# A ViT tower on one core: norms in two pieces, first tiles on the rounded input, and next query and key weights split at another place

## The reference, cut to what matters

```python
def t5_layer_norm(x, w):
    var = jnp.mean(x * x, axis=-1, keepdims=True)
    return w * x * jax.lax.rsqrt(var + EPS)
...
for i in range(L):
    nx = t5_layer_norm(h, ln1[i])
    q = (nx @ attn_q[i]).reshape(b, s, H, DK)
    k = (nx @ attn_k[i]).reshape(b, s, H, DK)
    v = (nx @ attn_v[i]).reshape(b, s, H, DK)
    scores = jnp.einsum('bqhd,bkhd->bhqk', q, k) + bias
    attn = jax.nn.softmax(scores, axis=-1)
    ctx = jnp.einsum('bhqk,bkhd->bqhd', attn, v).reshape(b, s, H * DK)
    h = h + ctx @ attn_o[i]
    nx = t5_layer_norm(h, ln2[i])
    y = jax.nn.relu(nx @ ffn_wi[i]) @ ffn_wo[i]
    if i in MOE_LAYERS:
        y = y + moe_ffn(nx.reshape(-1, d), gate_w[mi], moe_w1[mi], moe_w2[mi]).reshape(b, s, d)
        mi += 1
    h = h + y
return t5_layer_norm(h, ln_f)
```

## Time and profile before

| | |
|---|---|
| median of 3 runs | 741.36 us (739.84 to 741.7) |
| the profiled execution | 745.19 us, of which 743.4 us is the span from its first to its last instruction |
| PE busy | 678.4 us, 91% of the span, 6658 matmuls |
| DVE, ACT, POOL busy | 446.8, 405.0, 351.7 us |
| mean granted clock of PE | 0.963 |
| chain that ended last, by engine | PE 63%, DVE 11%, ACT 9%, POOL 8%, DMA 4%, issue 3% |

### The profile page before, as it was taken

The page is one execution under the profiler, slowest core; times in us unless marked ns, Lnnn a source line. Parts: engine busy times, 40 slices in busy tenths (PEclk is TensorE's granted clock), DMA queues, the critical chain, the costliest instruction groups (busy, mean ns, idle before and its releaser), DMA issues.

```text
span 743.4 us, 16264 instructions
## 1 busy us (share of the span) xinstructions
PE 678.4 (91%) x6658; PEld 609.8 (82%) x6658; DVE 446.8 (60%) x941; ACT 405.0 (54%) x914; POOL 351.7 (47%) x329
## 2 busy tenths in 40 slices
PE   6879979799889999999899989998899999999995
PEld 4757857588768888999899878787688898999994
DVE  0483567275475677565566655853856775666664
ACT  1486655534364374776675455444543647767642
POOL 2755275742573561547674424426734514553510
PEclk9998779988999999999999999989999999999998
DMA  9210100400221122434444110002211124333200
GB/s 256 75 48 7 40 1 2 118 2 1 77 74 44 33 72 64 134 109 128 134 118 122 42 45 2 2 1 75 76 44 33 61 75 134 90 104 107 75 1 23
DMA packets 36769, 49.20 MB, mean 66 GB/s; under 512 B 6315, under 2 KB 27735, under 8 KB 36183
## 3 DMA queue, kind: packets, MB, share of 16 engines
q1 hardware_dynamic: 33259, 43.49, 20.3%
q10 hardware_dynamic: 3436, 4.67, 2.1%
HBM read 47.70 MB, written 0.45 MB: 65 GB/s over the span
## 4 chain that ended last, share of the span: by engine, by line
PE 63%; DVE 11%; ACT 9%; POOL 8%; DMA 4%; issue 3%; ACTq 1%; SPq 0%; POOLq 0%; DVEq 0%
PE pd L716 31%; PE pa L716 21%; PE ps L716 7%; PE pa L747 4%; POOL prob L649 3%; POOL w L640 3%; ACT wide L1057 2%; DMA gate<-in_gate_w_dram 2%; DVE xn L1143 1%; DVE mx L1097 1%; ACT pa L1058 1%; DVE prob L1265 1%; POOL prob L655 1%; DVE xs L1109 1%; DVE xs L1107 1%
## 5 line engine op out<-in xcount | busy, mean ns | idle before, releaser
L640 POOL TENSOR_TENSOR w<-raw,w 128x384 fp32r<-128x384 f32 x140 | 141.7, 1014 | 126.3 <-ACT w L968 118.4
L716 PE MATMUL pd<-wide,w 128*128 128x264 f32 x1200 | 157.8, 288 | 0.1
L716 PEld LDWEIGHTS pd<-wide,w 128*128 128x128 f32 x1200 | 151.0, 190 | 1.0 <-DVE wide L1288 0.9
L716 PE MATMUL pa<-xs,w 128*128 128x264 f32 x810 | 121.2, 290 | 12.3 <-DVE wide L1288 8.1
L716 PEld LDWEIGHTS pa<-xs,w 128*128 128x128 f32 x810 | 107.7, 191 | 16.8 <-DVE wide L1288 10.2
L1288 DVE TENSOR_TENSOR wide<-pa,wide 128x264 fp32r<-128x264 f32 x144 | 62.0, 432 | 42.3 <-ACT pa L1058 40.2
L649 POOL TENSOR_TENSOR prob<-prob,mx 66x792 f32<-66x792 f32 x36 | 54.3, 1511 | 57.4 <-DVE mx L1097 57.1
L1057 ACT ACTIVATE wide<-pa 128x264 fp32r<-128x264 f32 x144 | 56.9, 395 | 38.1 <-PE pa L716 38.0
L655 POOL TENSOR_TENSOR prob<-prob,rc 66x792 f32<-66x792 f32 x36 | 54.3, 1511 | 45.1 <-DVE rc L1103 45.1
L716 PE MATMUL ps<-xs,w 128*128 128x264 f32 x480 | 74.2, 285 | 0.6 <-DVE prob L1265 0.6
L1179 DVE TENSOR_TENSOR pd<-pd,vtok 128x264 f32<-128x264 f32 x64 | 43.6, 681 | 41.5 <-PE pd L716 41.3
(11 more groups left out here) (139 smaller groups left out, 1101.0 us busy)
## 6 DMA issues: line engine op xcount, KB each, us to landing
raw<-in_moe_w_dram SPq DMA_DIRECT2D x16, 576.0 KB, 4.1
raw<-in_moe_w_dram SPq DMA_DIRECT2D x16, 384.0 KB, 3.5
raw<-in_moe_w_dram SPq DMA_DIRECT2D x32, 192.0 KB, 4.0
vtok<-cw_rows ACTq DMA_DIRECT2D x4, 1056.0 KB, 6.1
raw<-in_attn_o_dram SPq DMA_DIRECT2D x4, 576.0 KB, 4.0
raw<-in_ffn_wo_dram SPq DMA_DIRECT2D x4, 576.0 KB, 4.1
vtok<-in_patches_dram SPq DMA_DIRECT2D x2, 768.0 KB, 7.9
raw<-in_attn_q_dram SPq DMA_DIRECT2D x4, 384.0 KB, 3.8
```

Of the source, the lines that this page charges most:

```text
L640: ins = nc.gpsimd.tensor_tensor(low, whole, high.bitcast(F32), ALU.subtract)
L716: return nc.tensor.matmul(out_ap, lhsT, rhs, start=first, stop=last)
```

## The change

Three things are changed, and the number of matmuls on data stays the same.

1. A stage `tail_squares` stands ahead of `squares` in twelve norms: ACT squares the tail when its sum with the tail's part of the output is made, and the main part later; PE sums the tail's three pieces first and waits once more ahead of the main part's three.
2. `first_products` takes the place of the first three tiles of every `qk` for queries and of the first three of a layer's first hidden block: it claims three banks, runs the two matmuls of each tile that need only the rounded main input (a new semaphore `hi_ready`, signalled by the rounding), then waits for `x_ready` and runs the other three of each tile.
3. In layers 0 and 2 the rounding (`high`) of the next layer's query and key weights goes ahead of `scale` of the second norm, and their remainders (`low`) right behind it; the number of fillers changes from 1, 3, 6 to 2, 2, 3, 4 around it.

```diff
             yield ("o_main", 0, layer)
+            yield ("tail_squares", 0, "ln2")
             yield ("squares", 0, "ln2")
-            yield from warm(1)
+            yield from warm(2)
             yield ("pv", 1, layer, 1)
             yield ("tp", 1, layer, 2)
             yield ("norm", 0, "ln2", layer)
+            yield from warm(2)
             yield ("pv", 1, layer, 2)
             yield ("tp", 1, layer, 3)
+            yield ("high", None, "qkv", layer + 1, 0)
+            yield ("high", None, "qkv", layer + 1, 1)
             yield from warm(3)
             yield ("scale", 0, "ln2", layer)
+            yield ("low", None, "qkv", layer + 1, 0)
+            yield ("low", None, "qkv", layer + 1, 1)
             yield ("pv", 1, layer, 3)
-            yield from warm(6)
+            yield from warm(4)
             yield from hid(0, layer, 0)
-            yield ("split", None, "qkv", layer + 1, 0)
             yield from y(0, layer, 0)
...
             yield ("norm", 0, "ln1", layer + 1)
-            yield ("split", None, "qkv", layer + 1, 1)
             yield from warm(4)
...
+            def first_products(banks, w_hi, w_lo, hf, scale_stage, full):
+
+                n, x = x_ready_after(scale_stage), xs[hf]
+                tiles = [(bank, slice(m * 128, (m + 1) * 128)) for m, bank in enumerate(banks)]
+                pe.wait_ge(hi_ready, n)
+                for bank, cols in tiles:
+                    mm(bank, w_hi[:, 0, cols], x[:, 0], True, False)
+                    mm(bank, w_lo[:, 0, cols], x[:, 0], False, False)
+                pe.wait_ge(x_ready, n)
+                for bank, cols in tiles:
+                    mm(bank, w_hi[:, 0, cols], x[:, 1], False, False)
+                    mm(bank, w_hi[:, 1, cols], x[:, 2], False, False)
+                    mm(bank, w_lo[:, 1, cols], x[:, 2], False, True).then_inc(full, 1)
...
-                    pe.wait_ge(sq_ready, sq_no.next())
+                    n = sq_no.next()
                     bank = bank_d()
-                    for r in range(RT):
-                        cols = slice(r * RTN, (r + 1) * RTN)
-                        mm(bank[0:RTN, r:r + 1], sq[:, 0, cols], mean_w[:, 0:1], True, False)
-                        last = mm(bank[0:RTN, r:r + 1], sq[:, 1, cols], half_w[:, 0:1], False, True)
+                    for a, w in ((1, half_w), (0, mean_w)):
+                        pe.wait_ge(sq_ready, 2 * n - a)
+                        for r in range(RT):
+                            last = mm(bank[0:RTN, r:r + 1], sq[:, a, r * RTN:(r + 1) * RTN], w[:, 0:1], a == 1 and r == 0, a == 0 and r == RT - 1)
...
                     w = w1[ffn_no(layer, blk) % 2]
+                    if blk == part == 0:
+                        first_products([bank_h()[:, 0:NT] for _ in range(KT // 2)], w[:, 0], w[:, 1], hf,
+                                       ("scale", hf, "ln2", layer), h_full)
+                        continue
...
+                if stage[0] == "tail_squares":
+                    nc.scalar.activation(sq[:, 1, :], src[:, 1, :], ACT.Square).then_inc(sq_ready, 1)
+                elif [x[0] for x in order[:at] if x[0] in ("squares", "tail_squares")][-1:] == ["tail_squares"]:
+                    nc.scalar.activation(sq[:, 0, :], src[:, 0, :], ACT.Square).then_inc(sq_ready, 1)
+                else:
+                    nc.scalar.activation(sq[:, :, :], src, ACT.Square).then_inc(sq_ready, 2)
...
-                done(nc.vector.tensor_copy(z[:, 0:3:2, :], x[:, :, :]))
+                nc.vector.tensor_copy(z[:, 0:3:2, :], x[:, :, :]).then_inc(hi_ready, 1)
+                dve.wait_ge(hi_ready, splits.next())
```

More of the change, by code:

```diff
@@ L235, in stages @@
             yield ("o_main", 1, layer)
+            yield ("tail_squares", 1, "ln2")
             yield ("squares", 1, "ln2")
@@ L256, in stages @@
         yield ("y_main", 1, layer - 1, 0)
+        yield ("tail_squares", 1, "ln1")
         yield ("squares", 1, "ln1")
@@ L463, in vit_tower @@
         h1_ready = sem("h1_ready")
+        hi_ready = sem("hi_ready")
         sq_ready, rs_ready, x_ready = sem("sq_ready"), sem("rs_ready"), sem("x_ready")
@@ L474, in vit_tower @@
         order = list(stages())
-        chunks = [x[2:] for x in order if x[0] == "split"]
+        chunks = [x[2:] for x in order if x[0] in ("split", "high")]
         FFN = [(layer, blk) for layer in range(LAYERS) for blk in range(blocks_of(layer))]
@@ L669, in _ @@
                 name = stage[0]
-                if name == "split":
+                if name in ("split", "low"):
                     low_parts()
@@ L837, in _ @@
                     layer, i = stage[2:4]
+                    pe.wait_ge(chunk_split, chunks_until("qkv", layer, i))
                     if i == 0:
-                        pe.wait_ge(x_ready, x_ready_after(("scale", hf, "ln1", layer)))
-                    pe.wait_ge(chunk_split, chunks_until("qkv", layer, i))
-                    for m in range(KT):
+                        first_products([bank_a()[:, 0:NT] for _ in range(3)], wqkv[:, 0, 0], wqkv[:, 1, 0], hf,
+                                       ("scale", hf, "ln1", layer), a_full)
+                    for m in range(0 if i else 3, KT):
                         product(bank_a()[:, 0:NT],
@@ L902, in _ @@
                     layer, blk, part = stage[2:5]
-                    if blk == part == 0:
-                        pe.wait_ge(x_ready, x_ready_after(("scale", hf, "ln2", layer)))
                     if part == 0:
@@ L972, in squares @@
                 hf, kind = stage[1:3]
-                source = [x for x in order[:at] if x[0] in ("mean", "scale", "fold", "o_main", "y_main") and x[1] == hf][-1]
+                last = ("o_tail", "y_tail") if stage[0] == "tail_squares" else ("mean", "scale", "fold", "o_main", "y_main")
+                source = [x for x in order[:at] if x[0] in last and x[1] == hf][-1]
                 before = [x for x in order[:at] if x[0] == "norm"]
@@ L978, in squares @@
                 src = xn[hf][:, :, :] if kind in ("complex", "encoder") else hT[:, :, hf * NT:(hf + 1) * NT]
-                nc.scalar.activation(sq[:, :, :], src, ACT.Square).then_inc(sq_ready, 1)
+                if stage[0] == "tail_squares":
[4 more added lines that the diff above has]
+                    nc.scalar.activation(sq[:, :, :], src, ACT.Square).then_inc(sq_ready, 2)
             act.dma_start(oneh_sb, onehot).then_inc(in_bias, 16)
@@ L1003, in _ @@
                         copy_a(cq[hf][:, stage[2], j, :], sgn[:, 0:1] if stage[2] == 2 else None)
-                elif name == "squares":
+                elif name in ("squares", "tail_squares"):
                     squares(stage, at)
@@ L1075, in _ @@
             d_no, s_no, steps, maxes, sums = (Tally() for _ in range(5))
-            hid_no, eg_no = (Tally() for _ in range(2))
+            hid_no, eg_no, splits = (Tally() for _ in range(3))
             def done(ins):
```

3 lines of the change are left out of this document (2 added, 1 removed).

## The result

The changed kernel took 751.2 us (median of 4 runs, 749.41 to 754.32) against 740.6 us (4 runs, 739.26 to 741.7) in the same session: ratio 1.013, 95% interval 1.009 to 1.0169. Twelve more executions later gave 747.44 us, ratio 1.0069 (1.0038 to 1.0101). It is slower in both; I had forecast 740.1 us and a range up to 744.2. Executions over 1.5% above the fastest of their kernel (6 of 351) are left out of all ratios and means.

What follows compares the result with a forecast made beforehand. PE's list of work plus the places where PE waits was taken to bound the kernel. With the clock held the terms summed to -1.3 us, from 741.36 to 740.1 us; range 738.9 to 741.3, 8 in 10 within 737.4 to 744.2.

Steps and rivals of the forecast that it cites:

- the term for the second norms: Layers 0 and 2: first hidden tile read at about 176.6 against 176.89, -0.3 us each if the clock holds.
- the base under it: Terms were added to the profiled execution of 745.19 us, then scaled by 0.995 to the median of 741.36 us.
- first norm of layers 1, 3, root to query read: With POOL's splits moved away, PE's idle ahead of the query matmuls goes: -1.54 us each.
- claim in layer 1: Second half's first hidden tiles of layer 0, run in layer 1, wait for a third bank: +1.15 us.
- its own hidden tiles: Layer 1's own first hidden tiles wait for the third bank, freed near 261.9: +1.14 us.
- layer 3, PE's start to read: Hidden tiles inside layer 3: four more matmuls stand before ACT's first read, +0.49 us.
- layer 2's second-half query tiles: They wait for all of the values' copies, starting at 449.10 instead of 448.77: +0.36 us.
- second half's query tiles, layers 1 and 3: Starting on rounded input at the fillers' end saves about 0.22 us each, -0.45 together.
- layers 1 and 3's last norm: Squares in two pieces bring the root sooner, removing PE's wait of 0.21 us: -0.42 us together.
- The slower rival: Clock falls at gaps left by three-bank claims, 2.5 us each; one fall 742.6, more about 745 us; 17%.
- the clock falls at the second norms as before: Rival: fillers don't keep the clock in layers 0 and 2, +1.0 us each instead of -0.3; 742.7 us; 22%.
- the move of POOL's pieces: POOL's pieces leave layers 1 and 3's first norm for the second norm before, where remainders take 1.13 us: -3.1 us at first norms.

Runs made afterwards that it cites:

- d1: The changed kernel as it stands, run again for twelve more executions: 747.44 us, ratio 1.0069.
- b4: The kernel before with `first_products` alone, plus 6 fillers ahead of its claim in layers 1 and 3: 745.11 us, ratio 1.003.
- a0: The kernel before, unchanged, run again: 742.34 us, ratio 0.9998.
- a2: The kernel before with `first_products` and its calls alone: 747.97 us, ratio 1.0075.
- c1: The changed kernel with the fillers of before: 745.17 us, ratio 1.0067.
- b2: The kernel before with the moved splits alone, old fillers kept, POOL's low parts not held back: 741.85 us, ratio 0.999.
- a1: The kernel before with the squares and sums in two pieces alone: 743.81 us, ratio 1.0015.
- the gated version: The kernel before with moved splits, old fillers, POOL's low parts waiting for the second norm's scaled input: 739.73 us, ratio 0.9956; again 741.44 us, 0.9991.

## Why the prediction was wrong

**The step that failed is the term for the second norms, -0.3 each, and the base under it.** "I add terms to 745.19 and scale by 741.36/745.19 = 0.995" took the 3.8 us above the median for something spread evenly. It was not: the profiled execution had the 2.8 us fall at both second norms, and the median execution has it less often (7 of 12 places in the six traces that leave that norm's splits and fillers alone). I credited the change with removing it: "first tile at about 176.6, against 176.89: -0.3". The changed kernel's 8.11 us from root to read in d1, at full clock, are even a little less than the 8.4 that this meant. But they stand against 5.88 in an execution where the clock holds. The term is +2.2 there, at each of two places, not -0.3. In d1:

```profile
168.57 0.85 POOL L671 TENSOR_TENSOR rs<-var,exponent 88x3 f32<-88x3 f32 x1 [1.40 <-DVE var L1158]
...
176.68 0.39 ACT L1090 ACTIVATE wide<-pa 128x264 fp32r<-128x264 f32 x1 [3.02 <-PE pa L726]
```

Most other terms were sized well. Measured by the same two instructions on either side, at full clock; the last column is what reaches the next root on POOL, from root to root:

| term | forecast | measured | at the next root |
|---|---|---|---|
| first norm of layers 1, 3, root to query read (6.56 to 5.17) | -1.54 each | -1.39 each | -1.39 each |
| the same place, the query tiles behind the first (first products) | 0 | | -0.37 each |
| claim in layer 1, values to read (3.16 to 4.49, b4) | +1.15 | +1.33 | +1.18 |
| its own hidden tiles, values' copy to read (0.74 in the earlier trace rows to 2.11) | +1.14 | +1.37 | +1.34 |
| layer 3, PE's start to read (0.88 in the earlier trace rows to 1.37) | +0.49 | +0.49 | +0.34 |
| layer 3, second half's hidden tiles (3.16 to 3.35) | +0.10 | +0.19 | +0.19 |
| layer 2's second-half query tiles | +0.36 | +0.47 | +0.47 |
| second half's query tiles, layers 1 and 3 | -0.22 each | -0.38 each | -0.38 each |
| layers 1 and 3's last norm, to its root, and on to the gate's matmul | -0.21 each | -0.22 each | -0.02 each |
| second norm of layers 0, 2 (5.88 to 8.11) | -0.3 each | +2.23 each | +2.16 each |
| one more filler ahead of that norm's root (read in layer 2) | in the row above | | +0.22 each |

The last norm's term failed too: the root comes 0.22 us sooner, but the scaled input does not, since DVE has two other steps to do first, and PE waits 0.43 us for it and not 0.22. The last column sums to +4.0 us, where the runs at equal clock say +4.7 and +4.5. Against a base with both falls the same rows give 4.0 - 2 x 2.8 = -1.7; I had -1.3.

The base alone does not make up the loss. With a fall at 7 of 12 places it is worth 2 x 7/12 x 2.8 = 3.3 us, and 4.0 - 3.3 = +0.7 would still lie in my range. What the sum also left out is that the half clock did not go away with the falls: d1's twelve executions spent 50.7 us at it, those of a0 48.8. An estimate from the traces: 1.1 to 2.4 us for the fall at the claim, and 1.5 us in the output matmuls at 8 of 12 places, thus 2.0 for two, make it +3.8 to +5.1, where the medians of d1 and a0 differ by 5.1 us. The falls in the hidden tiles, in some of the traces, are not priced.

**The clock.** The slower rival named the right place and cause: the claim empties PE and the clock falls behind it. It did so in layer 1 in all four traces that have this claim without fillers (a2, c1, d1 and the changed kernel's first), behind 2.01 or 2.02 us of idle; in layer 3 the same claim leaves 0.91 us of idle, and the clock held in all four. I had given this rival 17%. d1's window:

```profile
214.70:221.30 6.60, 6.09 (x28) 6.12 (x29) 3.00 (x7) 3.56 (x11) 3.44 (x3) 0.50 0.01 2
```

Its price of 2.5 us fits the fall of 6.8 us in d1 (2.4) and was too high for those of 3.4 us (1.1), and the 1.50 us gap of the earlier trace rows that kept its clock was weak evidence against it: the gap here is 2.01 us. The rival "the clock falls at the second norms as before" asked whether the fillers keep the clock. With the new fillers the clock held up to the last 2.5 us ahead of the read in all six traces, and up to the read at 8 of 12 places; what I missed is that the fall then comes later, in work that is waited for. The Trainium skill (TensorE: Matmul & The Clock Gate, HAM oscillation) blames gaps between bursts of matmuls, in its case waits for a DMA. I had held the trace against it. Behind the claims the runs lean to it (a fall behind 2.01 us of idle, none with fillers in it), but the length of a gap alone does not decide: 2.12 us in b2's layer 2 kept the clock, and the falls inside a filler stretch with no gap stay unexplained by it. **What was right:** the move of POOL's pieces, their 1.13 us on the remainders, and that the rounding waits behind them.

**Still open:** what decides from one execution to the next whether the clock falls at a second norm or between 58 and 71 us; the price of the squares in two pieces (a1 includes zero, and their traces show no gain); and whether the gated version is a gain.

## What to carry to other kernels

Before terms are added to a profiled execution, ask where it differs from the median: if some stretch runs at half clock, take both values as bases, since a change can't be credited with removing what many executions never had, and a fall that is gone from one place can come at another. A function that claims all its buffers before its first instruction waits for the last one even where the old code overlapped that wait; claim them as they are used. Fillers that look redundant may be where the clock falls, under another engine's slow steps, so thin them only together with a look at what runs behind.

## What the runs showed of the hardware

The same kernel, unchanged, spread over 738.25 to 746.06 us in twelve executions, and most of it went with the granted clock: 0.32 us per us at half clock. A fall costs what the stretch behind it is worth: 2.8 us over six fillers that the next step stood behind, 1.1 us (2.4 when it lasted 6.8 us and not 3.4) in tiles paced by ACT, 1.4 to 1.6 us in output matmuls that the query tiles wait for, and 0.06 to 0.4 us in the same output matmuls when PE had a wait of 1.54 us behind them. PE's clock fell behind 2.01 us of idle in layer 1's claims, held through 2.12 us in b2, and fell with PE busy throughout in the fillers. Beside POOL's pieces DVE's remainder took 1.13 us and its rounding 1.07 us, against 0.43 us alone.
